# Cross attention of a Perceiver block: scores in sixteen 32 x 32 tiles, probabilities in three buffers and turned two steps behind, both maxima ahead of normalising

## The chip, the cores and the metric

The kernel runs on one core of one Trainium2 chip. The metric is the device time of one execution in microseconds (us). The kernel before took 2543.09 us (median of 3 runs, 2541.92 to 2548.95).

## The reference, cut to what matters

The block computes three residual parts one after the other: cross attention, self attention, and a mixture of 64 experts. The change touches the first alone.

```
x: (32, 32, 512)      ctx: (32, 257, 512)      16 heads of 32
q = heads(layernorm(x)); k = v = heads(ctx)
scores  = einsum('bhqd,bhkd->bhqk', q, k) / sqrt(32)
weights = softmax(scores)                       # over 257 keys
x = x + einsum('bhqk,bhkd->bhqd', weights, v)
x = x + self_attention(layernorm(x))
x = x + experts(layernorm(x))
```

There is no projection in the cross attention: queries are the normalised rows of x, keys and values are the context itself. All of it is in fp32.

## The kernel before, in words

Everything is written out by hand: each engine has its own instruction list, in the order of the code, and waits on semaphores; nothing plans or reorders it. The cross attention is the first block (lines 151 to 369).

First x comes in, is normalised (DVE), transposed (TensorE) and copied to XT (ScalarE, `copy_tiles`), with features on the partitions: XT[:, g, :] holds four heads (h = 0 to 3) in 32 partitions each, and g = 0 to 3 counts these groups.

Then a loop over the 32 batches. What happens to one batch b:

- SyncE loads K(b), 514 KB (line 206), and V(b) in two transfers of 384 and 130 KB (lines 209, 210), each into one of four buffers. Before K(b) it waits until scores(b-4) are done, before V(b) until values(b-4) are done. All of these stand in one list: K(b), V(b), V(b), K(b+1), and so on, and after batch 31 the loads of the weights W (line 212).
- GpSimd copies the 32 queries of each head into Q (line 235), a block diagonal 128 x 128 matrix for each g that was zeroed at the start (line 221), with four buffers.
- TensorE `scores(b)` (line 243): for each g one matmul with Q as weights (128 x 128) and K moving (257 columns), into PSUM bank g. Rows of the result are head and query, columns are keys. It waits until the exponential of the batch before has read bank g.
- DVE `largest(b, half)`: the maximum over 257 keys of two banks (line 336), times -scale (line 340), twice a batch.
- ScalarE: four exponentials out of PSUM into PR (line 316) with their sums.
- DVE `normalise(b)`: reciprocal (line 346) and one multiplication of all of PR (line 348).
- TensorE `turn(b)` (line 254): twelve transposes of PR into banks 4, 5 and 6 (lines 262, 263).
- ScalarE copies banks 4 and 5 to PTa (line 310), DVE copies bank 6 to PTb (line 356).
- TensorE `values(b)` (line 266): 48 matmuls with 32 columns of V as weights and 32 columns of PTa or PTb moving (line 281), into bank 7; DVE `place_out(b)` copies the result to AT (line 329).

The order of the steps on each engine is what the change edits. Before, in step b:

- TensorE: scores(b), values(b-3), turn(b-1)
- ScalarE: copy of turn(b-2) to PTa, exponentials of b
- DVE: copy of turn(b-2) to PTb, largest(b, 0), normalise(b-1), largest(b, 1), place_out(b-3)

PR, PTa, PTb and the small vectors have two buffers. After the loop AT is transposed back (line 298) and added to x (line 367), and the self attention starts with a conversion of W (line 567). A matmul in fp32 shows in the trace as two records of the matmul and two of the weight load.

Of the kernel before, what the change touches and what calls it, by code (L numbers as in the profile page):

```python
# [11 lines left out]
ACT = mybir.ActivationFunctionType  # L12
AX = mybir.AxisListType

P = 128
B = 32
SQ = 32
SK = 257
D = 512
G = D // P  # L20
# [13 lines left out]
KC = 96  # L34
KR = SK - 2 * KC
# [80 lines left out]
def program(nc, x, ctx_k, ctx_v, wq, wk, wv, wo, bq, bk, bv, bo, wg, shared, experts, out):  # L116
    root = ExitStack()
    with root:
# [5 lines left out]
        def sem(name):  # L124
            return root.enter_context(nc.semaphore(name))

        sb = allocator(root)
        ps = root.enter_context(nc.psum_tensor("ps", [P, 8, 512], F32))
# [3 lines left out]
        ident = sb("ident", [P, P])  # L132
# [18 lines left out]
        with ExitStack() as st:  # L151
            sb = allocator(st)
            XN = sb("a_XN", [P, TT, D])
            XT = sb("a_XT", [P, G, T])
            Q = sb("a_Q", [P, 4, G, P])
            K = sb("a_K", [P, 4, G, SK])
            V = sb("a_V", [P, 4, 3, D])
            PR = sb("a_PR", [P, 2, G, SK])
            PTa = sb("a_PTa", [P, 2, 2, G, P])
            PTb = sb("a_PTb", [KR, 2, G, P])  # L160
            AT = sb("a_AT", [P, G, T])
# [13 lines left out]
            xt_psum = sem("a_xt_psum")  # L175
            xt_copied = sem("a_xt_copied")
            made = sem("a_made")
            zeroed = sem("a_zeroed")
            ident_ready = sem("a_ident_ready")
            q_ready = sem("a_q_ready")  # L180
            s_done = sem("a_s_done")
            max_done = sem("a_max_done")
            nm_done = sem("a_nm_done")
# [34 lines left out]
            @block.gpsimd  # L218
            def _(pool):
                pool.memset(ident[:, :], 0.0).then_inc(made, 1)  # L220
                pool.memset(Q[:, :, :, :], 0.0).then_inc(zeroed, 1)
                pool.wait_ge(made, 1)
                pool.affine_select(out=ident[:, :], in_=ident[:, :], compare_op=ALU.not_equal, fill=1.0, base=0,
                                   pattern=[[-1, P]], channel_multiplier=1).then_inc(ident_ready, 1)
                pool.wait_ge(zeroed, 1)

                for b in range(B):
                    i = b % 4
                    if i == 0:
                        pool.wait_ge(xt_copied, b // 4 + 1)  # L230
                    if b >= 4:
                        pool.wait_ge(s_done, 2 * (b - 3))
                    for h in range(4):
                        r = slice(32 * h, 32 * h + 32)
                        pool.tensor_copy(Q[r, i, :, r], XT[r, :, SQ * b:SQ * (b + 1)]).then_inc(q_ready, 1)

            @block.tensor
            def _(pe):
                pe.wait_ge(ident_ready, 1)
                transpose_tiles(pe, ps, XN, ident, xn_ready, xt_psum, xt_copied)  # L240
                pe.wait_ge(xt_copied, TT)

                def scores(b):
                    i = b % 4
                    pe.wait_ge(q_ready, 4 * b + 4)
                    pe.wait_ge(k_in[i], 16 * (b // 4) + 16)
                    for g in range(G):
                        if b >= 1:
                            pe.wait_ge(exp_done, 4 * (b - 1) + g + 1)
                        last = pe.matmul(ps[:, g, 0:SK], Q[:, i, g, :], K[:, i, g, :], start=True, stop=True)  # L250
                        if g % 2 == 1:
                            last.then_inc(s_done, 1)

                def turn(b):

                    pe.wait_ge(pr_ready, b + 1)
                    if b >= 1:
                        pe.wait_ge(pta_ready, b)
                        pe.wait_ge(ptb_ready, b)
                    for g in range(G):  # L260
                        for k in range(2):
                            pe.transpose(ps[0:KC, 4 + k, g * P:(g + 1) * P], PR[:, b % 2, g, k * KC:(k + 1) * KC], ident[:, :])
                        last = pe.transpose(ps[0:KR, 6, g * P:(g + 1) * P], PR[:, b % 2, g, 2 * KC:SK], ident[:, :])
                    last.then_inc(t_done, 1)

                def values(b):

                    i = b % 4
                    pe.wait_ge(pta_ready, b + 1)
                    pe.wait_ge(ptb_ready, b + 1)  # L270
                    pe.wait_ge(v_in[i], 32 * (b // 4) + 32)
                    if b >= 1:
                        pe.wait_ge(at_ready, b)
                    for g in range(G):
                        for k in range(3):
                            for h in range(4):
                                r = slice(32 * h, 32 * h + 32)
                                w = slice(g * P + 32 * h, g * P + 32 * h + 32)
                                v = V[0:KC, i, k, w] if k < 2 else V[0:KR, i, 2, w]
                                pt = PTa[0:KC, b % 2, k, g, r] if k < 2 else PTb[:, b % 2, g, r]  # L280
                                last = pe.matmul(ps[r, 7, g * SQ:(g + 1) * SQ], v, pt, start=(k == 0), stop=(k == 2),
                                                 skip_group_check=True)
                    last.then_inc(pv_done, 1)

                for b in range(B + 3):
                    if b < B:
                        scores(b)
                    if b >= 3:
                        values(b - 3)
                    if 1 <= b <= B:  # L290
                        turn(b - 1)

                pe.wait_ge(at_ready, B)
                for t in range(TT):
                    if t >= 2:
                        pe.wait_ge(x1_ready, t - 1)
                    for g in range(G):
                        last = pe.transpose(ps[:, t % 2, g * P:(g + 1) * P], AT[:, g, t * P:(t + 1) * P], ident[:, :])
                    last.then_inc(back_psum, 1)

            @block.scalar
            def _(act):
                copy_tiles(act, ps, XT, small, ln_done, std_ready, xt_psum, xt_copied)

                for b in range(B + 2):
                    if b >= 2:
                        act.wait_ge(t_done, b - 1)
                        if b >= 4:
                            act.wait_ge(pv_done, b - 3)
                        act.activation(PTa[0:KC, b % 2, :, :, :].rearrange("p k g n -> p (k g n)"),  # L310
                                       ps[0:KC, 4:6, :].rearrange("p k n -> p (k n)"), ACT.Copy).then_inc(pta_ready, 1)
                    for g in range(G if b < B else 0):
                        act.wait_ge(nm_done, 2 * b + g // 2 + 1)
                        if b >= 2:
                            act.wait_ge(t_done, b - 1)
                        act.activation(PR[:, b % 2, g, :], ps[:, g, 0:SK], ACT.Exp, bias=nm[:, b % 2, g:g + 1],
                                       scale=SCALE, accum_out=sm[:, b % 2, g:g + 1]).then_inc(exp_done, 1)

            @block.vector
            def _(dve):  # L320
# [5 lines left out]
                def place_out(b):  # L326

                    dve.wait_ge(pv_done, b + 1)
                    dve.tensor_copy(AT[:, :, SQ * b:SQ * (b + 1)],
                                    ps[:, 7, 0:P].rearrange("p (g n) -> p g n", g=G)).then_inc(at_ready, 1)  # L330
# [11 lines left out]
                def normalise(b):  # L342

                    k = b % 2
                    dve.wait_ge(exp_done, 4 * b + 4)
                    dve.reciprocal(rs[:, k, :], sm[:, k, :]).then_inc(rec_done, 1)
                    dve.wait_ge(rec_done, b + 1)
                    dve.tensor_tensor(PR[:, k, :, :], PR[:, k, :, :], rs[:, k, :].rearrange("p (g o) -> p g o", o=1).to_broadcast([P, G, SK]),
                                      ALU.mult).then_inc(pr_ready, 1)

                for b in range(B + 3):
                    if 2 <= b < B + 2:
                        dve.wait_ge(t_done, b - 1)
                        if b >= 4:
                            dve.wait_ge(pv_done, b - 3)
                        dve.tensor_copy(PTb[:, b % 2, :, :].rearrange("p g n -> p (g n)"), ps[0:KR, 6, :]).then_inc(ptb_ready, 1)
                    if b < B:
                        largest(b, 0)
                    if 1 <= b <= B:
                        normalise(b - 1)  # L360
                    if b < B:
                        largest(b, 1)
                    if b >= 3:
                        place_out(b - 3)
                for t in range(TT):
                    dve.wait_ge(back_psum, t + 1)
                    dve.tensor_tensor(X[:, t, :], X[:, t, :], ps[:, t % 2, :], ALU.add).then_inc(x1_ready, 1)
# [1347 lines left out]
```

## Time and profile before

| | |
|---|---|
| median of 3 runs | 2543.09 us |
| profiled execution | 2544.21 us |
| its span | 2542.5 us |
| TensorE busy, share of the span | 96% |
| the loop over batches, from the first scores to the last copy of a result | 20.7 to 187.5 us |

The span is the time from the first to the last instruction of the profiled execution; what lies around it is 1.7 us. The share of TensorE is a mean over three very different stages, most of it over the experts (from 345 us on).

### The profile page before, as it was taken

How to read it: one execution, taken by the hardware profiler on the slowest of the kernel's cores; microseconds unless marked ns; L12 is line 12 of the kernel's file. 1: busy time of each engine (PE TensorE's matmuls, PEld its weight loads, DVE VectorE, ACT ScalarE, POOL GpSimd, SP SyncE). 2: the span in 40 equal slices, each digit the busy share in tenths (PEclk: the TensorE clock that was granted, in tenths of full speed). 3: DMA queues.
4: the chain of work that ended last, by engine and by line, in shares of the span. 5: the costliest groups of instructions: out<-in, count | busy, mean ns of one | idle time of the engine just before them, and what ended most of it. 6: DMA issues, size and time to landing. Idle time of an engine off the chain costs nothing.

```text
span 2542.5 us, 53551 instructions
## 1 busy us (share of the span) xinstructions
PE 2435.0 (96%) x22042; PEld 1994.8 (78%) x22042; DVE 1995.0 (78%) x1896; ACT 1690.0 (66%) x2119; POOL 639.5 (25%) x542
## 2 busy tenths in 40 slices
PE   6876989998999999999999999999999999999998
PEld 5765767776888888888888888888888888888886
DVE  6866557665799889998978988988778777767795
ACT  5642333334688778887867887877667767766784
POOL 3411010001132332332222233223222222222221
PEclk9987989998999999999999999999999999999999
DMA  6870022244899999998979999999888888887894
GB/s 201 224 221 0 2 106 110 86 161 166 300 378 381 362 344 384 375 374 332 375 288 326 367 355 351 385 356 344 303 296 325 327 300 325 326 296 280 311 372 133
DMA packets 128526, 714.99 MB, mean 281 GB/s; under 512 B 15488, under 2 KB 23808, under 8 KB 52416
## 3 DMA queue, kind: packets, MB, share of 16 engines
q1 hardware_dynamic: 102048, 665.96, 67.9%
q0 software_dynamic: 26144, 44.06, 8.3%
q8 instruction: 273, 4.47, 0.7%
q14 instruction: 61, 0.50, 0.1%
HBM read 684.46 MB, written 25.49 MB: 279 GB/s over the span
## 4 chain that ended last, share of the span: by engine, by line
PE 75%; issue 0%; DVE 0%; POOL 0%; ACT 0%; ACTq 0%; POOLq 0%; DVEq 0%
PE ps L1539 14%; PE ps L1541 14%; PE ps L1540 14%; PE ps L1617 7%; PE ps L1619 7%; PE ps L1618 7%; PE ps L1570 5%; PE ps L1589 4%; PE ps L1602 3%; PE ps L1527 1%; PE ps L1580 1%; PE ps L1530 0%; DVE e_WL L1430 0%; ACT e_WH L1348 0%; POOL out_rows L1501 0%
## 5 line engine op out<-in xcount | busy, mean ns | idle before, releaser
L1430 DVE TENSOR_TENSOR e_WL<-ring,e_WH 128x2048 fp32r<-128x2048 f32 x462 | 1057.3, 2289 | 234.0 <-ACT e_WH L1348 228.7
L1348 ACT ACTIVATE e_WH<-ring 128x2048 fp32r<-128x2048 f32 x462 | 885.1, 1916 | 125.1 <-PE ps L1541 56.9
L1539 PE MATMUL ps<-e_WH,e_XEh 128*128 128x512 f32 x1536 | 605.1, 394 | 3.6 <-DVE e_XEl L1452 3.6
L1541 PE MATMUL ps<-e_WH,e_XEl 128*128 128x512 f32 x1536 | 599.4, 390 | 0.0
L1540 PE MATMUL ps<-e_WL,e_XEh 128*128 128x512 f32 x1536 | 598.8, 390 | 0.0
L1489 POOL TENSOR_TENSOR e_tick<-e_tick 128x1 f32<-128x1 f32 x126 | 111.9, 888 | 1305.2 <-ACT X L1396 1184.6
L1539 PEld LDWEIGHTS ps<-e_WH,e_XEh 128*128 128x128 f32 x1536 | 289.0, 188 | 62.0 <-DVE e_XEl L1452 4.0
L1541 PEld LDWEIGHTS ps<-e_WH,e_XEl 128*128 128x128 f32 x1536 | 288.9, 188 | 61.2
L1540 PEld LDWEIGHTS ps<-e_WL,e_XEh 128*128 128x128 f32 x1536 | 289.1, 188 | 58.0
L1617 PE MATMUL ps<-e_WH,e_GTh 128*128 128x512 f32 x768 | 318.8, 415 | 0.0
L1430 DVE TENSOR_TENSOR e_WL<-e_more,e_WH 128x2048 fp32r<-128x2048 f32 x114 | 260.8, 2289 | 53.8 <-ACT e_WH L1348 52.5
L1619 PE MATMUL ps<-e_WH,e_GTl 128*128 128x512 f32 x768 | 301.7, 393 | 0.0
L1618 PE MATMUL ps<-e_WL,e_GTh 128*128 128x512 f32 x768 | 299.3, 390 | 1.1 <-issue 1.1
L1348 ACT ACTIVATE e_WH<-e_more 128x2048 fp32r<-128x2048 f32 x114 | 218.5, 1916 | 27.5 <-PE ps L1541 14.3
L1503 POOL DMA_INDIRECT out_rows<-X,lists x64 | 174.4, 2726 | 19.5 <-issue 19.5
L1619 PEld LDWEIGHTS ps<-e_WH,e_GTl 128*128 128x128 f32 x768 | 144.1, 188 | 33.9
L1618 PEld LDWEIGHTS ps<-e_WL,e_GTh 128*128 128x128 f32 x768 | 145.1, 189 | 26.4 <-issue 1.4
L1617 PEld LDWEIGHTS ps<-e_WH,e_GTh 128*128 128x128 f32 x768 | 144.5, 188 | 23.8 <-issue 0.4
L1356 ACT ACTIVATE X<-ps 128x512 f32<-128x512 f32 x192 | 115.3, 601 | 62.8 <-PE ps L1541 62.8
L1438 DVE TENSOR_TENSOR X<-X,ps 128x512 f32<-128x512 f32 x192 | 130.6, 680 | 4.0 <-PE ps L1541 4.0
L744 POOL DMA_INDIRECT XO<-xn_scratch,lists x64 | 127.1, 1986 | 19.5 <-issue 18.6
L1458 DVE TENSOR_TENSOR e_GTl<-ps,e_GTh 128x512 fp32r<-128x512 f32 x192 | 131.1, 683 | 0.0
(224 smaller groups left out, 3314.6 us busy)
## 6 DMA issues: line engine op xcount, KB each, us to landing
ring<-in_experts SPq DMA_DIRECT2D x462, 1024.0 KB, 8.3
e_more<-in_experts SPq DMA_DIRECT2D x114, 1024.0 KB, 8.4
ring<-in_shared SPq DMA_DIRECT2D x12, 1536.0 KB, 6.5
a_K<-in_ctx_k SPq DMA_DIRECT2D x32, 514.0 KB, 5.4
a_V<-in_ctx_v SPq DMA_DIRECT2D x32, 384.0 KB
a_V<-in_ctx_v SPq DMA_DIRECT2D x32, 130.0 KB
X<-in_x SPq DMA_DIRECT2D x4, 512.0 KB, 4.9
xn_scratch<-ring SPq DMA_DIRECT2D x1, 2048.0 KB, 7.4
```

Source lines behind the costliest of these rows:

```text
L1348: act.activation(WH[:, nth % HELD, :], unit(i), ACT.Copy).then_inc(hi_done, 1)
L1430: dve.tensor_tensor(WL[:, at, :], unit(place(kind, n)), WH[:, at, :], ALU.subtract).then_inc(lo_done, 1)
L1438: dve.tensor_tensor(GF[n % 2], SL[n % 2], up_ps, ALU.mult).then_inc(gf_done, 1)
L1458: dve.tensor_tensor(GTl[:, n % 2, :, :], turn_ps.rearrange("p (j n) -> p j n", j=G), GTh[:, n % 2, :, :], ALU.subtract).then_inc(gtl_done, 1)
L1503: pool.indirect_dma_start(out4, bass.IndirectOffsetOnAxis(lists[:, 1, e, 1:2], 0), Y2, None, compute_op=ALU.add).then_inc(added, 16)
L1539: pe.matmul(dst, h, wh, start=(k == 0), stop=False)
L1540: pe.matmul(dst, h, wl, start=False, stop=False)
L1541: last = pe.matmul(dst, l, wh, start=False, stop=(k == G - 1))
L1570: pe.matmul(over_ps[32 * c:32 * c + 32, kind * P:(kind + 1) * P], XEo[:, e % 2, k, :], w[:, k * D + c * P:k * D + (c + 1) * P], start=(kin ...
L1617: pe.matmul(down_ps, h, wh, start=(b == 0 and j == 0), stop=False)
L1618: pe.matmul(down_ps, h, wl, start=False, stop=False)
L1619: last = pe.matmul(down_ps, l, wh, start=False, stop=(b == NB - 1 and j == G - 1))
```

## The change

It touches the cross attention alone, and in it the lists of GpSimd, TensorE, ScalarE and DVE; the list of SyncE stays as it is.

- Q, its zeroing and its copies go. For each g and each head h there is now one matmul with 32 queries of XT as weights (32 rows, 32 columns) and the 32 rows of K of that head moving (257 columns). Its result goes to the 32 partitions `column(g, h)` = (g + h) mod 4 of bank g, so that over the four g all sixteen 32 x 32 tiles of the array are used. `values` reads the turned probabilities at the same place.
- PR has three buffers in place of two.
- Turning runs two steps behind the scores in place of one, copying three in place of two, and values and the placing of results four in place of three.
- DVE takes both maxima of b ahead of normalising b-1.

```diff
-            Q = sb("a_Q", [P, 4, G, P])
-            PR = sb("a_PR", [P, 2, G, SK])
+            PR = sb("a_PR", [P, 3, G, SK])
...
-                pool.memset(Q[:, :, :, :], 0.0).then_inc(zeroed, 1)
...
-                for b in range(B):
-                    i = b % 4
-                    if i == 0:
-                        pool.wait_ge(xt_copied, b // 4 + 1)
-                    if b >= 4:
-                        pool.wait_ge(s_done, 2 * (b - 3))
-                    for h in range(4):
-                        r = slice(32 * h, 32 * h + 32)
-                        pool.tensor_copy(Q[r, i, :, r], XT[r, :, SQ * b:SQ * (b + 1)]).then_inc(q_ready, 1)
...
+                def column(g, h):
+
+                    c = (g + h) % 4
+                    return slice(32 * c, 32 * c + 32)
+
                 def scores(b):
                     i = b % 4
-                    pe.wait_ge(q_ready, 4 * b + 4)
                     pe.wait_ge(k_in[i], 16 * (b // 4) + 16)
+                    at = slice(SQ * b, SQ * (b + 1))
                     for g in range(G):
                         if b >= 1:
                             pe.wait_ge(exp_done, 4 * (b - 1) + g + 1)
-                        last = pe.matmul(ps[:, g, 0:SK], Q[:, i, g, :], K[:, i, g, :], start=True, stop=True)
+                        for h in range(4):
+                            r = slice(32 * h, 32 * h + 32)
+                            last = pe.matmul(ps[column(g, h), g, 0:SK], XT[r, g, at], K[r, i, g, :], start=True, stop=True,
+                                             skip_group_check=True)
...
-                for b in range(B + 3):
+                for b in range(B + 4):
                     if b < B:
                         scores(b)
-                    if b >= 3:
-                        values(b - 3)
-                    if 1 <= b <= B:
-                        turn(b - 1)
+                    if b >= 4:
+                        values(b - 4)
+                    if 2 <= b <= B + 1:
+                        turn(b - 2)
...
+                for b in range(B + 3):
+                    if b >= 3:
+                        copy_turned(b - 3)
                     for g in range(G if b < B else 0):
                         act.wait_ge(nm_done, 2 * b + g // 2 + 1)
-                        if b >= 2:
-                            act.wait_ge(t_done, b - 1)
-                        act.activation(PR[:, b % 2, g, :], ...
+                        if b >= 3:
+                            act.wait_ge(t_done, b - 2)
+                        act.activation(PR[:, b % 3, g, :], ...
...
-                for b in range(B + 3):
-                    if 2 <= b < B + 2:
-                        dve.wait_ge(t_done, b - 1)
-                        ...
+                for b in range(B + 4):
+                    if 3 <= b < B + 3:
+                        copy_rest(b - 3)
                     if b < B:
                         largest(b, 0)
+                        largest(b, 1)
                     if 1 <= b <= B:
                         normalise(b - 1)
-                    if b < B:
-                        largest(b, 1)
-                    if b >= 3:
-                        place_out(b - 3)
+                    if b >= 4:
+                        place_out(b - 4)
```

`copy_turned(b)` and `copy_rest(b)` are the copies of before with their waits, for turn(b): first t_done for b, then, from b = 2 on, pv_done for b-2.

## Rows read from the trace of the kernel before

**Rows 1.** The page: busy us of each engine (share of the span, instructions).
```profile
PE 2435.0 (96%) x22042; PEld 1994.8 (78%) x22042; DVE 1995.0 (78%) x1896; ACT 1690.0 (66%) x2119; POOL 639.5 (25%) x542
```

**Rows 2.** One stretch: length, busy PE PEld DVE ACT POOL, granted clock, DMA share, GB/s.
```profile
33.08:165.00 131.92, 116.91 (x3166) 99.07 (x3168) 107.29 (x220) 81.11 (x248) 50.86 (x100) 1.00 0.79 216
```

**Rows 3.** SyncE's issues in time: start, us, instruction; L206 loads K, L209 V.
```profile
35.97 0.31 SPq L209 DMA_DIRECT2D a_V<-in_ctx_v  x1
...
36.80 0.35 SPq L206 DMA_DIRECT2D a_K<-in_ctx_k  x1
40.72 0.31 SPq L209 DMA_DIRECT2D a_V<-in_ctx_v  x1
...
165.85 0.31 SPq L209 DMA_DIRECT2D a_V<-in_ctx_v  x1
```

**Rows 4.** TensorE in time: start, us, what, records, idle before and releaser.
```profile
36.47 0.42 PE L262 MATMUL ps<-ident,a_PR 128*96 128x128 f32 x2 [0.53 <-DVE a_PR L348]
...
37.82 1.91 PE L250 MATMUL ps<-a_K,a_Q 128*128 128x257 f32 x8
39.66 0.33 PE L281 MATMUL ps<-a_PTa,a_V 96*32 96x32 f32 x16
...
40.44 0.25 PE L281 MATMUL ps<-a_PTb,a_V 65*32 65x32 f32 x6
41.28 0.42 PE L262 MATMUL ps<-ident,a_PR 128*96 128x128 f32 x2 [0.60 <-DVE a_PR L348]
```

**Rows 5.** Waits from 20 to 180 us: us in total, times, longest.
```profile
PE ps L250 <- POOL a_Q L235: 0.8, 1, 0.8
SPq L209 <- PE ps L281: 91.6, 28, 12.9
```

**Rows 6.** Issue to landing: all K; K(5); slowest K from 36 us on; last W.
```profile
DMA to landing us min/median/max: 3.5/5.4/13.7
DMA to landing us min/median/max: 5.5/5.5/5.5
DMA to landing us min/median/max: 6.1/6.1/6.1
W<-in_wo SPq DMA_DIRECT2D x1, 1024.0 KB, 12.1
```

**Rows 7.** DVE in time: the last result placed.
```profile
187.17 0.29 DVE L329 COPY a_AT<-ps 128x128 f32<-128x128 f32 x1 [4.08 <-PE ps L281]
```

**Rows 8.** TensorE's two long pauses, and stretches as in rows 2 (clock third from the end).
```profile
175.78 0.27 PE L281 MATMUL ps<-a_PTb,a_V 65*32 65x32 f32 x3 [2.67 <-issue]
337.82 0.66 PE L515 MATMUL ps<-ident,b_S 128*128 128x128 f32 x4 [2.46 <-DVE b_S L658]
...
338.00:340.00 2.00, 2.00 (x37) 1.45 (x37) 1.24 (x3) 0.20 (x1) 0.00 (x0) 0.77 0.04 8
340.00:342.00 2.00, 2.00 (x6) 1.52 (x6) 0.69 (x1) 1.95 (x4) 0.00 (x0) 0.50 0.00 0
342.00:344.00 2.00, 2.00 (x12) 1.39 (x14) 0.00 (x0) 0.68 (x2) 0.00 (x0) 0.88 0.00 0
```

**Rows 9.** TensorE in time at the lower clock: turning, then values, first and last.
```profile
176.68 0.66 PE L262 MATMUL ps<-ident,a_PR 128*96 128x128 f32 x2
...
179.40 0.44 PE L281 MATMUL ps<-a_PTa,a_V 96*32 96x32 f32 x16
...
183.24 0.45 PE L281 MATMUL ps<-a_PTa,a_V 96*32 96x32 f32 x16 [0.47 <-DVE a_AT L329]
...
184.40 0.33 PE L281 MATMUL ps<-a_PTb,a_V 65*32 65x32 f32 x5
```

**Rows 10.** TensorE in time: matmuls into strips and tiles of the array.
```profile
274.84 1.29 PE L506 MATMUL ps<-b_KT,b_QT 32*32 32x32 f32 x128
...
1501.46 1.08 PE L1570 MATMUL ps<-ring,e_XEo 128*32 128x128 f32 x32
1502.36 1.06 PE L1570 MATMUL ps<-e_more,e_XEo 128*32 128x128 f32 x32
```

More of the change, by code:

```diff
@@ L177, in program @@
             made = sem("a_made")
-            zeroed = sem("a_zeroed")
             ident_ready = sem("a_ident_ready")
-            q_ready = sem("a_q_ready")
             s_done = sem("a_s_done")
@@ L224, in _ @@
                                    pattern=[[-1, P]], channel_multiplier=1).then_inc(ident_ready, 1)
-                pool.wait_ge(zeroed, 1)
-                for b in range(B):
-                    i = b % 4
-                    if i == 0:
-                        pool.wait_ge(xt_copied, b // 4 + 1)
-                    if b >= 4:
-                        pool.wait_ge(s_done, 2 * (b - 3))
-                    for h in range(4):
-                        r = slice(32 * h, 32 * h + 32)
-                        pool.tensor_copy(Q[r, i, :, r], XT[r, :, SQ * b:SQ * (b + 1)]).then_inc(q_ready, 1)
             @block.tensor
@@ L261, in turn @@
                         for k in range(2):
-                            pe.transpose(ps[0:KC, 4 + k, g * P:(g + 1) * P], PR[:, b % 2, g, k * KC:(k + 1) * KC], ident[:, :])
-                        last = pe.transpose(ps[0:KR, 6, g * P:(g + 1) * P], PR[:, b % 2, g, 2 * KC:SK], ident[:, :])
+                            pe.transpose(ps[0:KC, 4 + k, g * P:(g + 1) * P], PR[:, b % 3, g, k * KC:(k + 1) * KC], ident[:, :])
+                        last = pe.transpose(ps[0:KR, 6, g * P:(g + 1) * P], PR[:, b % 3, g, 2 * KC:SK], ident[:, :])
                     last.then_inc(t_done, 1)
@@ L279, in values @@
                                 v = V[0:KC, i, k, w] if k < 2 else V[0:KR, i, 2, w]
-                                pt = PTa[0:KC, b % 2, k, g, r] if k < 2 else PTb[:, b % 2, g, r]
+                                q = column(g, h)
+                                pt = PTa[0:KC, b % 2, k, g, q] if k < 2 else PTb[:, b % 2, g, q]
                                 last = pe.matmul(ps[r, 7, g * SQ:(g + 1) * SQ], v, pt, start=(k == 0), stop=(k == 2),
@@ L303, in _, with copy_turned @@
                 copy_tiles(act, ps, XT, small, ln_done, std_ready, xt_psum, xt_copied)
-                for b in range(B + 2):
+                def copy_turned(b):
+                    act.wait_ge(t_done, b + 1)
                     if b >= 2:
-                        act.wait_ge(t_done, b - 1)
[L308 to L311, printed above, removed]
+                        act.wait_ge(pv_done, b - 1)
+                    act.activation(PTa[0:KC, b % 2, :, :, :].rearrange("p k g n -> p (k g n)"),
+                                   ps[0:KC, 4:6, :].rearrange("p k n -> p (k n)"), ACT.Copy).then_inc(pta_ready, 1)
+                for b in range(B + 3):
+                    if b >= 3:
+                        copy_turned(b - 3)
                     for g in range(G if b < B else 0):
                         act.wait_ge(nm_done, 2 * b + g // 2 + 1)
-                        if b >= 2:
-                            act.wait_ge(t_done, b - 1)
-                        act.activation(PR[:, b % 2, g, :], ps[:, g, 0:SK], ACT.Exp, bias=nm[:, b % 2, g:g + 1],
+                        if b >= 3:
+                            act.wait_ge(t_done, b - 2)
+                        act.activation(PR[:, b % 3, g, :], ps[:, g, 0:SK], ACT.Exp, bias=nm[:, b % 2, g:g + 1],
                                        scale=SCALE, accum_out=sm[:, b % 2, g:g + 1]).then_inc(exp_done, 1)
@@ L347, in normalise, with copy_rest @@
                     dve.wait_ge(rec_done, b + 1)
-                    dve.tensor_tensor(PR[:, k, :, :], PR[:, k, :, :], rs[:, k, :].rearrange("p (g o) -> p g o", o=1).to_broadcast([P, G, SK]),
+                    dve.tensor_tensor(PR[:, b % 3, :, :], PR[:, b % 3, :, :], rs[:, k, :].rearrange("p (g o) -> p g o", o=1).to_broadcast([P, G, SK]),
                                       ALU.mult).then_inc(pr_ready, 1)
-                for b in range(B + 3):
-                    if 2 <= b < B + 2:
-                        dve.wait_ge(t_done, b - 1)
-                        if b >= 4:
-                            dve.wait_ge(pv_done, b - 3)
-                        dve.tensor_copy(PTb[:, b % 2, :, :].rearrange("p g n -> p (g n)"), ps[0:KR, 6, :]).then_inc(ptb_ready, 1)
+                def copy_rest(b):
+                    dve.wait_ge(t_done, b + 1)
+                    if b >= 2:
+                        dve.wait_ge(pv_done, b - 1)
+                    dve.tensor_copy(PTb[:, b % 2, :, :].rearrange("p g n -> p (g n)"), ps[0:KR, 6, :]).then_inc(ptb_ready, 1)
+                for b in range(B + 4):
+                    if 3 <= b < B + 3:
+                        copy_rest(b - 3)
                     if b < B:
                         largest(b, 0)
+                        largest(b, 1)
                     if 1 <= b <= B:
                         normalise(b - 1)
-                    if b < B:
-                        largest(b, 1)
-                    if b >= 3:
-                        place_out(b - 3)
+                    if b >= 4:
+                        place_out(b - 4)
                 for t in range(TT):
```

## The prediction

> **What bounds the kernel now.** The page comes first [rows 1]: TensorE is busy for 96% of the span, but that is the mean over stages. The change touches only the cross attention, so I read the windows of that stage. Its loop runs from 20.7 to 187.5 us [rows 7], 7% of the span, and in its steady part (33 to 165 us, [rows 2]) TensorE is busy 89% of the time, VectorE 81%, ScalarE 61%, the DMA engines 79%. A gain or loss here moves the later stages in time and does not change them.
>
> One batch takes 4.81 us: SyncE issues the first half of V for batch 4 at 35.97 and for batch 31 at 165.85, 27 steps in 129.88 us [rows 3]. The timeline of TensorE fills one step [rows 4]: scores start at 37.82, values at 39.66 (1.84 us), their last record ends at 40.44 + 0.25 = 40.69 (1.03 us), then 0.60 us of waiting for the normalised probabilities, then turning from 41.28, which lasts as long as the one before it (36.47 to 37.82, 1.35 us). Sum 4.82. So TensorE is the limit, with one wait of 0.6 us, on VectorE's a_PR. In the view of waits nothing on TensorE waits for K or V.
>
> How near K is to being late decides this case. SyncE's queue is served in order: K(b), wait for values(b-4), V(b), V(b), K(b+1). Before V it waits for the value matmuls 28 times, 91.6 us in all [rows 5]: once for each of batches 4 to 31. So K(b+1) leaves 0.83 us after V(b) (35.97 to 36.80), right after values(b-4), although its own slot has been free since scores(b-3). Before, values(b-4) stand in TensorE's step b-1 and K(b+1) is needed at step b+1: K(5) is issued at 36.80 and needed at about 42.6. It lands 5.5 us after its issue, at 42.3 [rows 6]. The slack is 0.3 us. The least of all is 3.5 us: K(4), alone in a quiet queue.
>
> **The change, part by part.**
>
> *Values one step later, and SyncE's queue as it was.* In the new order TensorE's step b is scores(b), values(b-4), turn(b-2). SyncE still waits for values(b-4) before V(b), and K(b+1) still stands behind V(b). Now only turn(b-2), 1.35 us, lies between that release and scores(b+1), which need K(b+1). Before, a whole step of 4.81 us lay there besides. So this closes a loop: end of values(b-4), V, V and K issued, K landed, scores(b+1), values(b-3). Its length with TensorE at full clock:
> - release to V: 40.69 to 40.72, 0.03 us [rows 3, 4];
> - V to K issue: 0.83 us [rows 3];
> - K issue to landing with both V in front in a queue that was empty, exactly K(5)'s case: 5.5 us. Bounds 3.5 (K alone) and 6.1 (the slowest from 36 us on), median 5.4 [rows 6];
> - landing to start: no row shows it on TensorE; semaphore to start on SyncE is the 0.03 us above, so 0;
> - scores 1.84, values 1.03.
>
> Sum 9.23 us. Turning (1.35 us) fits in the 6.36 us of the wait, and so do maxima, exponentials, normalising and both copies: VectorE's and ScalarE's whole load of a step is 3.9 us and 3.0 us (0.81 and 0.61 of 4.81, [rows 2]). All their new slack is thus worth nothing: TensorE waits for K. The loop holds for K(5) to K(31), 27 steps; K(4) is not behind a values wait.
>
> *TensorE's clock.* In the loop TensorE works 1.84 + 1.03 + 1.35 = 4.2 us and then idles 5.0 us, each step. The granted clock stayed at 1.00 from 33 to 165 us with a pause of 0.6 us each step [rows 2, 4], but around pauses of 2.67 us (173 to 175.8) and 2.46 us (to 337.8) it fell to 0.50 [rows 8], the lower of its two levels (1.2 GHz against 2.4). A pause of 5 us is longer than both. So I expect each step to begin at 1.2 GHz. What that costs comes from rows at that level: turning takes 2.72 us (176.68 to 179.40) where it took 1.35, so scores 3.68; 93 of the 96 value records take 1.49 us (183.24 to 184.73), so values 1.5 [rows 9]. Loop: 3.68 + 1.5 + 0.03 + 0.83 + 5.5 = 11.5 us. After the second pause the lower level lasted 3.4 us (three stretches of 2 us at a mean of 0.77, 0.50 and 0.88: 0.92 + 2.0 + 0.48) and was gone while TensorE worked [rows 8]; a step's work at half clock is 3.68 + 1.5 + 2.72 = 7.9 us, so it rises inside the step, sometimes before scores and values (5.2 us) are through. If at the earliest 3.4 us into them, (5.2 - 3.4)/2 = 0.9 us comes back, if late nothing; I take half: 11.1 us. The Trainium skill, "TensorE: Matmul & The Clock Gate", section "HAM oscillation — how this bites in real kernels", tells of the same form, bursts of about 2 us between DMA waits of 3 to 5 us with a cold start of every burst; by it the loop would be near the 11.5 us of the upper bound, and the rows above bear the direction out.
>
> *Scores in sixteen 32 x 32 tiles.* Four matmuls of 257 columns become sixteen with 32 rows and 32 columns of weights each; four of one g have different rows and columns of the array. The nearest rows for size: sixteen matmuls into four column strips, 128 columns moving, take 0.90 us (1501.46 to 1502.36) [rows 10]; two records a matmul there, as here. One plain matmul of 257 columns takes 1.84 / 4 = 0.46 us, so one of 128 columns 0.229; sixteen of them took 0.90, four at a time (0.225 us). Four tiles of 257 columns then take 0.225 x 257/128 = 0.45 us, and 16 matmuls 1.81 us, as 1.84 before. Bounds: 1.7 and, if the tiles don't overlap at all, 4 x 1.84 = 7.4. I take no change. The Trainium skill speaks against it: "TensorEngine Tiling (Array Packing)", "Gotcha 1: PSUM Pressure", says that different row tiles cannot access one PSUM bank at once, and here all four write bank g. The row against it: L506 puts 64 matmuls of 32 x 32, four rows of tiles into one bank, in 1.29 us, 20 ns each [rows 10]; a lone one of 32 columns would cost 0.46 x 32/257 = 57 ns, so about three ran side by side. The trace disagrees with the page; its case is the second rival.
>
> *Edits at nothing.* POOL's zeroing and its 128 copies into Q go: TensorE waited for them 0.8 us once [rows 5]; otherwise they lay beside scores three batches away. Both maxima ahead of normalising, and the third PR buffer, remove the 0.6 us a_PR wait; under the loop it is not on the path. Even if it were, it would be worth 0.6 x 27 = 16 us.
>
> *Ends of the stage.* Before the loop there are four steps without values; they have 1.84 + 1.35 us of TensorE's work and lasted about the 4.8 us of the others [rows 4]. Three steps give back between 0 and 1.6 us each: I take -3 us. At the end one more step is needed. Before, V(31) is issued at 165.85 and the last result stands at 187.46, much of it at half clock already [rows 3, 7, 9]. One values (1.5) more, and half clock for scores(31) (1.84) and turn(29) (1.35) as well: +5 us, bounds 0 and +10. W's loads follow V(31) in the queue; the last landed 12.1 us after its issue [rows 6], and some 20 us of this stage lie behind that point before and after: still covered.
>
> **Sum.** 27 x (11.1 - 4.81) = 170; -3 + 5 = +2. The profiled execution took 2544.2 us (span 2542.5): 2716. The median of the timed runs is 1.1 lower: 2715.
>
> **The rivals.**
> 1. *The clock stays up.* Same loop at 9.23 us: 27 x 4.42 = 119, in all 2665. For it: pauses of 0.6 us did nothing, and two falls are few to judge by [rows 2, 8]. Against: this pause is 5 us in one piece, each step. 14%.
> 2. *The tiles run one after the other* (the bank). Scores 7.4 us: loop 14.8 at full clock, 27 x 10 = 270, 2816; some 2860 with part at half clock. Against: [rows 10]. 5%.
> 3. *Faster: K is in time.* Then the step is TensorE's 1.84 + 1.03 + 1.35 = 4.22 us: 27 x -0.59 = -16, less 3, plus 5: 2530. The place is K's landing; it decides once K(b+1) lands within 1.35 us of the end of values(b-4), that is 0.5 us after its issue. The least seen is 3.5 [rows 6], and each us beyond costs 27 us; break-even needs a loop of 4.7 us, of which scores and values leave 1.8 for three issues and a landing. Only a queue that does not hold K behind V could do it. 2%.
>
> **Chances and range.** The forecast (slower by the loop, part of it at half clock) 79%. Its own range: landing 5.0 to 6.1 (27 x -0.5 to +0.6), clock share 10.6 to 11.5: 2690 to 2742. 80% range with rival 1: 2660 to 2745. What this kernel's timing can tell from no change is about 0.3%, 8 us: slower by more than that 97%, within it 1%, faster 2%.
>
> **What the profile after would show.** Right: TensorE idle 4 to 6 us before scores with nothing of an engine as releaser (a DMA, or issue), V issued every 11 us, K landing about 5.5 us after its issue, DMA share of the stage down from 0.79 to about 0.35, a granted clock that alternates between 0.5 and 1.0, scores records that span 1.8 us at full clock. Wrong: a step near 9.2 us with the clock at 1.00 (rival 1); scores lasting 7 us (rival 2); K's issue not tied to values, a step near 4.3 us (rival 3).

## The result, and the profile after

The changed kernel takes 2647.15 us (median of 6 runs, 2641.56 to 2653.57), the kernel before 2543.14: a ratio of 1.0405, 95% interval 1.0387 to 1.0423. It is slower, as forecast, but by 104 us where 172 were forecast, and below the range (2660 to 2745). The profiled execution has a span of 2651.8 us (before 2542.5).

The page and the steady stretch of the loop, as in [rows 1, 2] (the granted clock is the third figure from the end):

```profile
PE 2456.3 (93%) x22810; PEld 1996.5 (75%) x22810; DVE 1994.8 (75%) x1896; ACT 1689.7 (64%) x2119; POOL 575.6 (22%) x413
...
33.00:270.00 237.00, 136.78 (x3815) 102.36 (x3813) 105.01 (x220) 81.98 (x250) 0.00 (x0) 0.65 0.42 122
```

TensorE is busy 58% of the loop (before 89%), the DMA engines 42% (before 79%), at a mean clock of 0.65. Something makes all of them wait. The waits, as in [rows 5], 33 to 270 us for TensorE and 20 to 300 for SyncE:

```profile
PE ps L243 <- DMA a_K<-in_ctx_k: 100.2, 27, 5.2
...
SPq L206 <- PE ps L276: 207.7, 28, 13.3
```

The first row is the loop of the prediction: scores (now L243) wait for K 27 times, 3.7 us each, where before they never did. SyncE still waits for values before V 28 times. In the list of issues in time the step is the distance from one V to the next, as in [rows 3]:

```profile
36.05 0.31 SPq L206 DMA_DIRECT2D a_V<-in_ctx_v  x1
36.40 0.92 SPq L207 DMA_DIRECT2D a_V<-in_ctx_v  x1
37.37 0.35 SPq L203 DMA_DIRECT2D a_K<-in_ctx_k  x1
44.68 0.31 SPq L206 DMA_DIRECT2D a_V<-in_ctx_v  x1
...
156.85 0.31 SPq L206 DMA_DIRECT2D a_V<-in_ctx_v  x1
...
271.67 0.31 SPq L206 DMA_DIRECT2D a_V<-in_ctx_v  x1
```

(271.67 - 36.05) / 27 = 8.73 us, before 4.81: 27 x 3.92 = 106 us, which is the whole loss. One step of TensorE in time, as in [rows 4]:

```profile
154.18 1.18 PE L243 MATMUL ps<-a_K,a_XT 32*32 32x257 f32 x32 [4.09 <-DMA a_K<-in_ctx_k]
155.28 0.44 PE L276 MATMUL ps<-a_PTa,a_V 96*32 96x32 f32 x16
...
156.48 0.32 PE L276 MATMUL ps<-a_PTb,a_V 65*32 65x32 f32 x8
156.72 0.66 PE L256 MATMUL ps<-ident,a_PR 128*96 128x128 f32 x2
...
163.19 1.18 PE L243 MATMUL ps<-a_K,a_XT 32*32 32x257 f32 x32 [3.67 <-DMA a_K<-in_ctx_k]
```

Values end at 156.80, V is issued at 156.85, the next scores start at 163.19. The surprise is the first row: sixteen score matmuls are through in 1.10 us (154.18 to 155.28), and that at the lower clock. Here is that clock around this step, and the durations of all score records with the landings of K:

```profile
152.00:154.00 2.00, 0.00 (x0) 0.00 (x0) 0.00 (x0) 0.00 (x0) 0.00 (x0) 0.66 0.57 218
154.00:156.00 2.00, 1.82 (x85) 1.01 (x88) 0.61 (x1) 0.00 (x0) 0.00 (x0) 0.50 0.00 0
156.00:158.00 2.00, 2.00 (x66) 1.91 (x58) 1.90 (x6) 1.68 (x7) 0.00 (x0) 0.50 0.14 22
158.00:160.00 2.00, 1.52 (x8) 1.08 (x6) 1.07 (x3) 0.70 (x3) 0.00 (x0) 0.63 0.76 230
160.00:162.00 2.00, 0.00 (x0) 0.00 (x0) 0.24 (x1) 0.58 (x1) 0.00 (x0) 1.00 0.84 268
...
L243 PE MATMUL ps<-a_K,a_XT x1024: 372/630/633, 21.4 to 269.5; 32*32 32x257 f32 x171
...
DMA to landing us min/median/max: 4.1/4.8/16.1
```

The clock rises after scores and values are done and falls again while TensorE waits. The median score record lasts 630 ns, those at the upper clock 372. In each of the 27 steps of the loop the first score record is one of the long kind.

The ends of the stage: scores(4) start at 33.24 (before 37.82), scores(31) at 269.0 (167.68), and the last result is placed at:

```profile
291.99 0.29 DVE L328 COPY a_AT<-ps 128x128 f32<-128x128 f32 x1 [3.81 <-PE ps L276]
```

So -4.6 ahead of the loop, and 23.3 us in place of 19.8 behind it: -1.1 in all, where +2 was forecast.

### The profile page after: what moved, and what is told of

Read it like the earlier page. It is cut to its first block, busy times and chain, and to the rows that moved or that the text cites. A ratio compares the mean times of both kernels' runs of the same rounds, so it can differ in the third digit from the quotient of the medians.

```text
span 2651.8 us, 54946 instructions
## 1 busy us (share of the span) xinstructions
PE 2456.3 (93%) x22810; PEld 1996.5 (75%) x22810; DVE 1994.8 (75%) x1896; ACT 1689.7 (64%) x2119; POOL 575.6 (22%) x413
## 4 chain that ended last, share of the span: by engine, by line
PE 72%; issue 0%; DVE 0%; POOL 0%; ACT 0%; ACTq 0%; POOLq 0%; DVEq 0%
PE ps L1541 13%; PE ps L1543 13%; PE ps L1542 13%; PE ps L1619 7%; PE ps L1621 7%; PE ps L1620 7%; PE ps L1572 5%; PE ps L1591 3%; PE ps L1604 3%; PE ps L1529 1%; PE ps L1582 1%; PE ps L1532 0%; DVE e_WL L1432 0%; ACT e_WH L1350 0%; POOL out_rows L1503 0%
## 5 line engine op out<-in xcount | busy, mean ns | idle before, releaser
L1620 PEld LDWEIGHTS ps<-e_WL,e_GTh 128*128 128x128 f32 x768 | 145.1, 189 | 28.4 <-issue 3.4
L315 ACT ACTIVATE a_PR<-ps,a_nm 128x257 f32<-128x257 f32 x128 | 59.1, 474 | 133.1 <-DVE a_nm L339 133.1
L243 PE MATMUL ps<-a_K,a_XT 32*32 32x257 f32 x1024 | 39.7, 592 | 103.4 <-DMA a_K<-in_ctx_k 100.2
```

The source lines that it names most:

```text
L1620: pe.matmul(down_ps, h, wl, start=False, stop=False)
```

## The experiments

**One step of the sum alone: the tiles in place of four full matmuls.** Two kernels take the scores apart from the loop. The first keeps the tiles but lets all four g use the four tiles on the diagonal:

```diff
-                    c = (g + h) % 4
+                    c = h
```

> The changed kernel with column(g, h) = h: every g uses the same four tiles on the diagonal of the array, in place of all sixteen over the four g. In the changed kernel the sixteen score matmuls of a batch took 1.10 us at the lower clock, where the prediction had 3.68. Theory A (all sixteen tiles run side by side, one tile's matmul after another only on the same tile): the four g now follow each other, scores take four times 0.86 to 0.92 us, 3.4 to 3.7 us at the lower clock, the loop grows from 8.73 to about 11.2 us and the time from 2647 to about 2710 us. Theory B (a matmul of 32 rows and 32 columns is itself shorter than the prediction had it, whatever its neighbours): scores stay near 1.1 us and the time at 2647 us.

Measured: 2706.24 us, ratio to the kernel before 1.0639 (1.0622 to 1.0656). The step is (328.09 - 35.92) / 27 = 10.82 us.

```profile
149.95 3.36 PE L243 MATMUL ps<-a_K,a_XT 32*32 32x257 f32 x32 [4.90 <-DMA a_K<-in_ctx_k]
153.24 0.44 PE L276 MATMUL ps<-a_PTa,a_V 96*32 96x32 f32 x16
```

The same 32 records take 3.3 us where they took 1.10. So it is not the small size of a matmul that makes the scores short: sixteen of them, on sixteen different tiles, run largely side by side. Theory A holds. The second has the full matmuls of before in the new order of steps:

```diff
-                        for h in range(4):
-                            r = slice(32 * h, 32 * h + 32)
-                            last = pe.matmul(ps[column(g, h), g, 0:SK], XT[r, g, at], K[r, i, g, :], ...
+                        last = pe.matmul(ps[:, g, 0:SK], Q[:, i, g, :], K[:, i, g, :], start=True, stop=True)
```

> The kernel before with the new order of steps alone (turning two behind, values four behind, three PR buffers, both maxima first); scores as four full matmuls with Q. Theory A (the loop was foreseen rightly and only the scores term was mis-sized): the loop is that of the changed kernel, 8.73 us, with scores of 3.5 to 3.7 us at the lower clock in place of 1.10: 11.2 us, less some tenths where the clock rises inside the step; time 2700 to 2715 us. Rival (with full matmuls TensorE works long enough to keep the upper clock): scores 1.84 us, values 1.03, loop about 9.0 us, time about 2655 us.

Measured: 2702.19 us, ratio 1.0623 (1.0607 to 1.0639), step 10.73 us. This is nearly the loop that was forecast (11.1 us), with the scores that it assumed:

```profile
149.33 3.77 PE L250 MATMUL ps<-a_K,a_Q 128*128 128x257 f32 x8 [4.05 <-issue]
153.03 0.44 PE L281 MATMUL ps<-a_PTa,a_V 96*32 96x32 f32 x16
...
160.48 3.01 PE L250 MATMUL ps<-a_K,a_Q 128*128 128x257 f32 x8 [4.50 <-issue]
163.42 0.44 PE L281 MATMUL ps<-a_PTa,a_V 96*32 96x32 f32 x16
```

3.70 us all at the lower clock in one step, 2.94 in the next, where the clock rose on the way: the part that the prediction took off. Here the view calls the wait for K "issue"; it is one for K all the same, since all 27 end 0.09 us after K has landed.

**The loop alone.** One kernel moves K ahead of V's wait in SyncE's list, and nothing else; one moves values and the placing of results back to three steps behind.

```diff
-                for b in range(B):
...
+                for b in range(B + 1):
+                    if b < B:
+                        i = b % 4
+                        if b >= 4:
+                            sp.wait_ge(s_done, 2 * (b - 3))
+                        sp.dma_start(K[:, i, :, :], ctx_k[b]).then_inc(k_in[i], 16)
+                    if b == 0:
+                        continue
+                    i = (b - 1) % 4
+                    if b >= 5:
+                        sp.wait_ge(pv_done, b - 4)
...
```

> The changed kernel with K(b+1) issued before the wait for V(b)'s buffer; nothing else differs. Theory A (K(b+1) behind V(b) closes a loop through values, issue, landing and scores): the loop now spans two steps (6.1 + 0.6 + 1.0 us, 3.9 a step) and no longer decides; the step is DVE's work of 3.9 us and its waits, 4.1 to 4.4 us, no wait of 4 us for a_K is left, the clock stays at 1.00, and the time is 2544 - 27 x 0.55 - 3, about 2526 us (2518 to 2536). Rival (it is the depth of the pipeline, three PR buffers and the later values, or the DMA engines' rate that costs the time): the step stays near 8.7 us, 2647 us.

Measured: 2545.68 us, ratio 1.0004 (0.9995 to 1.0013): the whole loss is gone, so the loop was its cause. But the gain of 18 us that theory A added did not come. The median step is 4.51 us, but the mean is 4.92 (4.81 before), since three steps take 7.5, 8.1 and 8.6. One of them, and TensorE's waits from 33 to 160 us:

```profile
90.38 0.31 SPq L210 DMA_DIRECT2D a_V<-in_ctx_v  x1
...
93.82 0.66 PE L260 MATMUL ps<-ident,a_PR 128*96 128x128 f32 x2 [2.69 <-issue]
...
98.52 0.31 SPq L210 DMA_DIRECT2D a_V<-in_ctx_v  x1
...
PE ps L247 <- DMA a_K<-in_ctx_k: 15.9, 16, 1.7
PE ps L280 <- issue: 7.3, 9, 2.9
PE ps L260 <- issue: 5.0, 2, 2.7
```

TensorE stands still in the middle of turning, with no engine and no load that released it, and runs at the lower clock behind that. Such waits are called "issue" below; what they go with is shown at the end of the experiments.

The second kernel of the pair has values (and the placing of results) three steps behind:

```diff
-                for b in range(B + 4):
+                for b in range(B + 3):
                     if b < B:
                         scores(b)
-                    if b >= 4:
-                        values(b - 4)
+                    if b >= 3:
+                        values(b - 3)
```

> The changed kernel with values and the placing of results three steps behind as before, the rest of the change kept, SyncE's list as it is. Theory A (the one step of delay of values is what closes the loop): the loop spans two steps again (6.1 + 0.65 + 1.04 = 7.8 us for two), the wait of 4 us for a_K goes, but values(b-3) now wait for the copy of turn(b-3) behind scores; step 4.4 to 4.9 us, time 2535 to 2550 us. Rival (the deeper order of PR and turning costs it): above 2600 us.

Measured: 2547.84 us, ratio 1.0023 (1.0009 to 1.0036). By this ratio it is some 6 us above the kernel before (2 to 9 by the interval), where the changed kernel is 104 above it: the one step of delay of values was nearly the whole of the loss. The deeper turning, the third buffer and all else that is left of the change come to these 6 us together; no run takes them apart.

**The clock's share.**

```diff
                     if 2 <= b <= B + 1:
                         turn(b - 2)
+                    if 5 <= b + 1 < B:
+                        pe.wait_ge(at_ready, b - 3)
+                        for n in range(34):
+                            pe.transpose(ps[:, 7, 2 * P:3 * P], ident[:, :], ident[:, :])
```

> The changed kernel with 34 transposes of the identity added after turn in each step of the loop, into columns of bank 7 that nothing reads, so that TensorE works through most of its wait for K; they change no result. Theory A (the wait lets the clock fall, and scores and values run at the lower one): the clock stays at 1.00, scores take 0.65 us for 1.10 and values 1.04 for 1.44, the loop falls from 8.73 to about 7.9 us, time 2647 - 27 x 0.85 = 2624 us. Rival (the dummies delay the scores, or the clock is not in the loop): 2647 us or more.

Measured: 2625.89 us, ratio 1.033 (1.0314 to 1.0346); 21 us come back by adding work. The stretch and one step:

```profile
33.00:250.00 217.00, 188.52 (x4669) 163.43 (x4667) 102.27 (x220) 78.51 (x250) 0.00 (x0) 1.00 0.45 131
...
91.65 0.73 PE L243 MATMUL ps<-a_K,a_XT 32*32 32x257 f32 x32 [1.21 <-DMA a_K<-in_ctx_k]
92.30 0.34 PE L276 MATMUL ps<-a_PTa,a_V 96*32 96x32 f32 x16
```

The clock is 1.00, scores take 0.65 us. The step is 8.13 us in the mean, for 8.73. The 21 us are a lower bound for what the clock costs: a wait for K is left in 8 steps only (4.5 us), in the others the added transposes themselves end last (7.92 us again and again).

**What the tiles alone do in the kernel before.** The first kernel has the order of steps of before, with `column`, XT and the loops of `scores` and `values` as in the change; the second is the same with K one batch ahead of V.

```diff
-                        last = pe.matmul(ps[:, g, 0:SK], Q[:, i, g, :], K[:, i, g, :], start=True, stop=True)
+                        for h in range(4):
+                            r = slice(32 * h, 32 * h + 32)
+                            last = pe.matmul(ps[column(g, h), g, 0:SK], XT[r, g, at], K[r, i, g, :], ...
```

> The kernel before with the sixteen tiles alone (no Q), the order of steps as before. Theory A (sixteen side by side, scores about 0.6 us at full clock): TensorE's step falls by 1.2 us, but the chain scores(b), first maximum, normalising b-1, turning b-1 (0.6 + 0.7 + 0.2 + 0.2 + 1.25 + 1.35 us) gives about 4.35 us a step, and K, two steps ahead, lands in 6.2 + values and scores over two steps, 3.9 us a step: step 4.35 to 4.5 us, time about 2532 us (2526 to 2538). Rival (scores are not what bounds the step, or K is late at once): the step stays at 4.8 us or more, 2543 us or above.

> The kernel before with the sixteen tiles and K issued one batch ahead of V (the tiles alone gave 2553 us: steps of 4.4 us and several of 6 to 8 us). Theory A (what the tiles alone lose is K's lateness at a shorter step): no wait for a_K, step about 4.4 us, 2535 us. Rival (it is lost at the issue waits of 3 us and the slower clock behind each of them, which K's place does not touch): 2548 us or more.

Measured: 2552.6 us, ratio 1.003 (1.0018 to 1.0042), and 2548.92 us, ratio 1.0023 (1.0012 to 1.0034). Theory A was wrong in both; the rivals hold. The first kernel's median step is 4.80 us, with five between 6.3 and 8.3; the second's 4.59 with three of 7.8 to 8.1, each again with an issue wait. 1.2 us less work on TensorE a step gains nothing here: both kernels are a little slower than the one before.

**Towards a faster version.** K two batches ahead of V; the same with the full matmuls; and the first without most of V's loads (the last two lines of the cut are in this third kernel alone).

```diff
-                for b in range(B):
+                AHEAD = 2
+                for c in range(B + AHEAD):
...
+                    b = c - AHEAD
...
                     if b >= 4:
-                        sp.wait_ge(pv_done, b - 3)
+                        continue
```

> The changed kernel with K issued two batches ahead of V (one ahead gave 2546 us, with 16 waits for a_K of up to 1.7 us left and three steps of 7.5 to 8.6 us in which TensorE stood still for 3 us at an issue wait). Theory A (both are real: the K waits go, the issue waits stay): 16 us of K waits go, of which some return as waits for DVE; step 4.5 us with the long ones, time 2535 us (2530 to 2541). Rival (the DMA engines' rate limits the step, K's distance doesn't matter): same as one ahead, 2543 to 2548 us.

> The new order of steps (turning two behind, values four behind, three PR buffers, both maxima first) with the four full score matmuls of before, and K issued two batches ahead of V. TensorE runs 24 matmul records less a step than with the tiles, and its step is 1.84 + 1.03 + 1.35 = 4.22 us. Theory A (with the tiles the steps of 8 us are TensorE waiting for its instructions, since it runs through more of them in less time): no step above 6 us, step 4.25 to 4.4 us, clock at 1.00, time 2544 - 27 x 0.45 - 3 = 2529 us (2524 to 2535). Rival (the long steps come with any step below 4.8 us): some steps of 8 us, 2540 us or more.

> The changed kernel with K two batches ahead, and V loaded for the first four batches only; later batches use those buffers again, so that half of the DMA traffic of the loop is left out and the result is not that of the reference. Theory A (TensorE's issue waits of 2 to 3 us are instruction fetches that come late because the DMA engines are full, 79% busy): the DMA share falls to about 0.4, the issue waits go, no step above 6 us, step 4.1 to 4.2 us as DVE allows, time about 2524 us (2518 to 2530). Rival (the issue waits are in TensorE's own sequence): they stay, time 2540 us or more.

Measured: 2543.48 us, ratio 1.0003 (0.9993 to 1.0013); 2540.66 us, ratio 0.9976 (0.9965 to 0.9986); 2533.49 us, ratio 0.995 (0.9934 to 0.9965). The first has no wait for K left and gained nothing measurable for it. The second, full matmuls in the new order with the queue mended, is the one real version that beats the kernel before, by some 6 us (4 to 9). Its common step is 4.15 us (4.22 was worked out for TensorE), but steps of 7.35, 6.92 and 8.53 eat most of that; 2529 was expected. The third was to show whether the issue waits are instruction fetches held up by full DMA engines. TensorE's waits of the first, of the second (36 to 165 us) and of the third (the first and the third from 33 to 165 us), and a stretch of the first and of the third:

```profile
PE ps L282 <- issue: 17.5, 15, 2.5
PE ps L249 <- issue: 4.4, 3, 2.0
PE ps L262 <- issue: 4.2, 2, 2.4
PE ps L263 <- issue: 2.8, 1, 2.8
...
36.00:150.00 114.00, 89.30 (x3211) 66.69 (x3204) 85.92 (x184) 66.76 (x207) 0.00 (x0) 0.88 0.77 211
```

```profile
PE ps L287 <- issue: 9.4, 7, 4.1
PE ps L256 <- issue: 2.1, 2, 1.3
```

```profile
PE ps L282 <- issue: 21.5, 19, 3.4
PE ps L262 <- issue: 3.1, 2, 1.8
PE ps L249 <- issue: 2.7, 4, 1.2
PE ps L263 <- issue: 1.1, 1, 1.1
...
36.00:150.00 114.00, 88.67 (x3385) 65.83 (x3399) 92.54 (x198) 72.31 (x224) 0.00 (x0) 0.93 0.47 150
```

The DMA engines are busy 47% (77% with V's loads), and the issue waits are all there: 28.4 us in 26 waits, against 28.9 in 21. A full DMA queue is not what they need. The time fits neither theory (2518 to 2530, or 2540 and more). Without V's loads the mean step is 4.61 against 4.88 us, some 7 us in all, and the last result is placed at 176.1 us, against 190.1; about half of these 14 us thus lies in the loop, most of the rest behind it.

**What the issue waits go with.** The trace records the packets of every DMA queue. One queue, q8, carries only packets of 16 KB of the kind "instruction", and in most of these loops one comes every 4 to 5 us. In the step shown above for K one batch ahead, TensorE is idle from 91.13 to 93.82; the packets of q8 between 90.8 and 92.4 us (count, MB, share of the DMA engines) are one, which runs from 91.33 to 92.23:

```profile
q8 instruction: 1, 0.02, 3.5%
```

It is so every time. The seven kernels of this part in which TensorE's wait for K is gone or short (K one and two ahead, values three behind, the tiles alone and with K ahead, and the last two) have 105 issue waits from 33 to 165 us, and each ends 1.2 to 1.8 us after such a packet is through, 2.2 to 3.7 us after it started. The 27 waits for K that the view calls "issue" in the kernel with full matmuls do not: each ends 4.1 us or more after the last such packet. So the first half of that theory A, that TensorE waits for its instructions, fits all 105; the second half falls, as those packets take 1.04 us in the mean without V's loads and 1.20 with them, and the waits stay. This is read from the times alone: the packets do not name their engine, no run changed the instructions or how they come in, and why a packet is sometimes late stays open. The kernel before has only two issue waits from 33 to 165 us, of 0.2 us each and not behind such a packet. In its last steps, from 175 us on, it has three that are, the 2.67 us of [rows 8] among them.

## Why the prediction was wrong, step by step

- *The loop through K's landing*: right. 27 waits for a_K; moving K ahead of V takes the whole loss away, moving values back all but some 6 us of it.
- *Its terms*: values to V 0.03 forecast, 0.05 to 0.06 measured. V to K 0.83 forecast, 1.09 measured as the mean of 27, since the second V takes 0.6 to 1.5 us to issue in 12 of them and 0.42 in the others; 0.83 was one step's, and the mean of the kernel before is 1.05 already. Landing 5.5 forecast, 4.92 the mean, inside the bounds (two of 27 above them, 6.6). Together 6.0 for 6.3. K landed to scores 0 forecast, 0.04 measured. Values 1.5 forecast, 1.51 measured. One reading was wrong, without harm: the least landing, 3.5 us, is not K(4)'s alone; K(13), behind both V, has it too.
- *Scores "I take no change"*: this step failed. The term was 1.84 us at the upper clock and 3.68 at the lower; it is 0.65 and 1.10. The forecast range for it, 1.7 to 7.4 us, did not hold the value, and 27 x (3.68 - 1.10) = 70 us is the gap: 2715 - 70 = 2645. That this comes so near to 2647 is in part luck: landing (-0.6 us a step), V to K (+0.3) and the recovery of the clock (+0.4, below) nearly cancel, and the ends of the stage take 3 us off. The row that sized it, matmuls into four column strips, could only show four side by side, because each takes all 128 rows of the array; I scaled it to tiles of 32 rows and 32 columns, of which sixteen fit. The rotation in `column` was in the code to be read: no tile is used twice in a batch. With it taken away, the forecast term came (3.3 us), and with full matmuls the forecast loop (10.73 for 11.1). The Trainium skill, "TensorEngine Tiling (Array Packing)", section "Theoretical Speedup", gives up to 4 for one small dimension and up to 16 for both. The two ratios measured, 1.84 / 0.65 = 2.8 against the four full matmuls, which do the same sixteen products, and 3.3 / 1.10 = 3.0 against the diagonal, which has four tiles, do not contradict it; no run here has one tile alone, against which the 16 would count.
- *The rule against the tiles* ("Gotcha 1: PSUM Pressure" of the same page of the Trainium skill: different row tiles cannot access one PSUM bank at once): the trace was right to overrule it for this form. Four row tiles write one bank in every g, each into 32 partitions of its own. If they took turns, the four would last 4 x 0.46 = 1.84 us (0.46 is one matmul of 257 columns); all sixteen are through in 0.65.
- *The clock*: right in kind, and its level at the start of the steps was the lower one in all 27. "I take half" of a recovery inside scores and values was for scores of 3.68 us; with the short ones nothing comes back, since in all 27 steps scores take 1.10 and values 1.51 us, both at the lower clock. The clock's worth is at least 21 us of the 104.
- *Ends of the stage* +2 forecast, -1 measured: -4.6 ahead (forecast -3), +3.5 behind (+5).
- *Rival 1* (clock stays up) fell, though its 2665 was near by accident. *Rival 3*: even with K in time the tiled kernel is no faster, because of the issue waits (28.9 us, all that TensorE waits for from 33 to 165 us with K two batches ahead), which no step of mine foresaw, though the first of them stood in [rows 8].

## What to carry to other kernels

When a step is moved later in a software pipeline, look at every wait in every queue that names its semaphore, above all a DMA queue served in order: what stands behind the wait is delayed too, though it needs nothing of that step. Before sizing a tiled matmul, list which tile of the array each one uses over the whole group; those on different tiles run together, those on one tile in turn, and a row of full-height matmuls bounds neither. And when the engine that bounds a step gets faster by a quarter, expect the next limit to be one that the profile of before hardly shows: here a few long waits called "issue" in the last steps of the loop were its only sign.

## What the runs showed of the hardware that was not expected

- Sixteen fp32 matmuls of 32 x 32 x 257 on sixteen tiles: 0.65 us at the upper clock, 1.10 at the lower; on four tiles 3.3 us at the lower.
- Once the common step is under 4.8 us, TensorE stands still at "issue" 6 to 26 times in the loop, for up to 4.1 us with full matmuls and 3.4 with tiles, with DMA engines busy 47% as with 77%. All 105 such waits of seven kernels end 1.2 to 1.8 us after a 16 KB packet of the instruction queue q8 is through.
- 34 useless transposes a step made a waiting kernel 21 us faster.
